# Loop 1 of a two-layer graph network: node sums over 32 nodes for each pair of tiles, in place of 128 nodes for each step of eight tiles

## The reference

```python
# layer 0, for each edge e from src to dst; w from a small MLP of the edge's length
w  = mlp(emb(edge_weight)).reshape(-1, 4, 32)
Y1 = sqrt(3) * edge_vec / |edge_vec|            # the edge's direction, 3 components
ss, vv = xs[src], xv[src]                       # 32 scalars, 32 vectors of 3
m0 = w[:, 0] * ss
m1 = w[:, 1][:, :, None] * ss[:, :, None] * Y1[:, None, :]
m2 = w[:, 2][:, :, None] * vv
m3 = w[:, 3] * einsum('emc,ec->em', vv, Y1) / sqrt(3)
msg_s = segment_sum(concat([m0, m3], 1), dst)   # sums over the edges of a node
msg_v = segment_sum(concat([m1, m2], 1), dst)
x = layernorm(x + concat([msg_s @ W_out0, msg_v . W_out1]) / 16)
```

## Time and profile before

| | |
|---|---|
| median of 3 runs | 2822.83 us (2813.37 to 2848.79) |
| profiled execution | 2817.75 us |
| its span, first to last instruction | 2815.9 us |
| mean granted clock of TensorE | 0.799 of full speed |
| TensorE matmul / weight load busy | 1998.1 / 1548.5 us |
| VectorE, ScalarE, GpSimd busy | 1563.1, 818.1, 1632.6 us |
| loop 1, by VectorE's first and last L805 | 70 to 1423 us |

### The profile page before, as it was taken

One profiled execution on the slowest core, in us unless ns is written; L12 is line 12 of the kernel. 1 busy time (PEld: TensorE's weight loads), 2 busy tenths in 40 slices (PEclk: granted clock), 3 DMA queues, 4 the chain that ended last, 5 costly groups with the idle time before them and its releaser, 6 DMA issues. The chain is left out here.

```text
span 2815.9 us, 38846 instructions
## 1 busy us (share of the span) xinstructions
PE 1998.1 (71%) x10027; PEld 1548.5 (55%) x10027; DVE 1563.1 (56%) x3820; ACT 818.1 (29%) x1930; POOL 1632.6 (58%) x1680
## 2 busy tenths in 40 slices
PE   6776878788888787888866556665566666566666
PEld 3554555555556465656545445555556555555555
DVE  6564455445445454556445436665566666566666
ACT  5111112112112112112124324343344434334443
POOL 6665654556656465566644555566556666665662
PEclk7787888888878888889877877777777777777878
DMA  8311222212222122222246543443343434333441
GB/s 265 92 44 37 60 56 63 60 54 63 59 59 65 50 60 56 67 60 71 69 119 166 135 120 89 93 94 92 86 97 94 95 91 95 92 88 93 95 97 46
DMA packets 221609, 238.19 MB, mean 85 GB/s; under 512 B 73212, under 2 KB 163240, under 8 KB 221131
## 3 DMA queue, kind: packets, MB, share of 16 engines
q0 software_dynamic: 53472, 110.50, 17.2%
q1 hardware_dynamic: 79835, 71.35, 8.3%
q10 hardware_dynamic: 88256, 55.83, 8.0%
HBM read 191.88 MB, written 45.62 MB: 84 GB/s over the span
## 5 line engine op out<-in xcount | busy, mean ns | idle before, releaser
L731 POOL DMA_INDIRECT gx<-node_d,idx x815 | 821.8, 1008 | 557.2 <-issue 245.5
L731 POOL DMA_INDIRECT gp<-p_tab_d,idx x831 | 787.8, 948 | 567.4 <-issue 281.8
L1096 PEld LDWEIGHTS ps_a<-hot,msg 128*128 128x128 f32 x3324 | 457.2, 214 | 205.7 <-issue 189.9
L1096 PE MATMUL ps_a<-hot,msg 128*128 128x128 f32 x3324 | 485.0, 302 | 52.2 <-issue 43.6
L2128 PE MATMUL ps_e<-win,hot_x 128*128 128x129 f32 x1664 | 319.8, 359 | 253.7 <-issue 163.3
L2128 PEld LDWEIGHTS ps_e<-win,hot_x 128*128 128x128 f32 x1664 | 289.1, 264 | 285.3 <-issue 199.5
L192 ACT ACTIVATE h<-ps_h,b 128x512 f32<-128x512 f32 x208 | 142.9, 687 | 750.1 <-remote 435.3
L2265 DVE TENSOR_TENSOR hot_x<-key_row,ps_s 128x1024 f32<-128x1024 bf16 x104 | 126.4, 1216 | 308.5 <-remote 263.1
L2217 PE MATMUL ps_g<-hot,hid 128*128 128x128 f32 x1664 | 239.5, 294 | 73.5 <-issue 71.5
L2013 ACT ACTIVATE hid<-hid,score 128x128 f32<-128x128 f32 x832 | 277.5, 393 | 10.1
L2217 PEld LDWEIGHTS ps_g<-hot,hid 128*128 128x128 f32 x1664 | 229.0, 209 | 90.0 <-issue 82.9
(11 more groups left out here) (303 smaller groups left out, 2425.4 us busy)
## 6 DMA issues: line engine op xcount, KB each, us to landing
win<-q_tab_d ACTq DMA_DIRECT2D x408, 64.5 KB
key_row<-key_row_d ACTq DMA_DIRECT2D x100, 256.0 KB
gp<-p_tab_d,idx POOLq DMA_INDIRECT x831
gx<-node_d,idx POOLq DMA_INDIRECT x815
p_tab_d<-acc SPq DMA_DIRECT2D x23, 516.0 KB
q_tab_d<-unit_area SPq DMA_DIRECT2D x36, 258.0 KB
q_tab_d<-acc SPq DMA_DIRECT2D x5, 774.0 KB, 4.1
emb<-emb_d SPq DMA_DIRECT2D x102, 32.0 KB
```

The costliest lines, as they stand in the source:

```text
L731: e.indirect_dma_start(out=buf[:, h, t, :], out_offset=None, in_=table, in_offset=bass.IndirectOffsetOnAxis(ap=idx[:, h, t:t + 1], axis=0) ...
L1096: last = e.matmul(ps_a[:, h, b, :], msgs[h].tile(t, b), hot[:, h, t, :], start=t == tiles.start, stop=t == tiles.stop - 1)
```

## The change

- The one-hot matrix of a tile is 32 wide (`WIN`) and not 128, and is made from `k["dloc"]`, which is relative to the start of the edge's pair.
- The matmuls of `sums` have 32 moving columns and not 128; the pair t // 2 has its own 32 columns of the half's 128 in the same bank, and each pair is a group of accumulation of its own.
- `add` loads four starts and adds four blocks of 2 x 32 columns to the accumulator, each waiting for the one before (`pair_own`), where it added one block of 2 x 128. The last step's two parts add two pairs each.
- `w["dloc"]`, its one subtraction in `prepare` and its count of edges outside go; layer 2's count, with the same blocks, is taken for both.

```diff
-        dloc=m.sb("dloc0", [P, LTILES]),
...
-                own.did(e.tensor_tensor(w["dloc"][:].rearrange(pairs, t=TPS), dstf[:].rearrange(pairs, t=TPS),
-                                        spread(of_step, 2, TPS), ALU.subtract))
...
-        hot = m.sb("hot0", [P, 2, TPS, P])
+        hot = m.sb("hot0", [P, 2, TPS, WIN])
...
                 def sums(h, b, tiles=slice(0, TPS)):
                     for t in range(tiles.start, tiles.stop):
-                        last = e.matmul(ps_a[:, h, b, :], msgs[h].tile(t, b), hot[:, h, t, :], start=t == tiles.start,
-                                        stop=t == tiles.stop - 1)
+                        last = e.matmul(ps_a[:, h, b, t // 2 * WIN:(t // 2 + 1) * WIN], msgs[h].tile(t, b), hot[:, h, t, :],
+                                        start=t % 2 == 0, stop=t % 2 == 1 or t == tiles.stop - 1)
...
                 def one_hot(j, h):
-                    e.tensor_tensor(hot[:, h], spread(ps_a[:, h, IOTA, :], 1, TPS),
-                                    spread(w["dloc"][:, bass.ds(j * TPS, TPS)], 2, P), ALU.is_equal)
-
-                def add(j, h, part=0):
-
-                    e.load([reg], k["start"][0:1, bass.ds(j * PPS, 1)])
-                    at = acc[:, :, bass.ds(e.snap(reg, min_val=0, max_val=N), P)]
+                    e.tensor_tensor(hot[:, h], spread(ps_a[:, h, IOTA, 0:WIN], 1, TPS),
+                                    spread(k["dloc"][:, bass.ds(j * TPS, TPS)], 2, WIN), ALU.is_equal)
+
+                def add(j, h, part=0, pairs=range(PPS)):
+
+                    starts = run_starts(e, k, j, regs)
                     e.wait_ge(sum_mm, j + (1 + part))
-                    e.wait_ge(acc_own, j + (2 + part))
-                    e.tensor_tensor(at, at, ps_a[:, h, 0:2, :], ALU.add).then_inc(acc_own, 1)
+                    for p in pairs:
+                        at = acc[:, :, bass.ds(starts[p], WIN)]
+                        if p == pairs.start:
+                            e.wait_ge(acc_own, j + (2 + part))
+                        else:
+                            e.wait_ge(pair_own, j * (PPS - 1) + (p - part))
+                        last = e.tensor_tensor(at, at, ps_a[:, h, 0:2, p * WIN:(p + 1) * WIN], ALU.add)
+                        last.then_inc(acc_own if p == pairs.stop - 1 else pair_own, 1)
...
-                in_block(own_w, w["dloc"], P)
                 messages(0, 3)
-                count(own_w, 0)
                 messages(1, 0)
-                in_block(own_w, k["dloc"], WIN)
+                in_block(own_w)
                 messages(1, 1)
-                count(own_w, 1)
+                count(own_w)
```

More of the change, by code:

```diff
@@ L608, in _ @@
                 pairs = "p (g t) -> p g t"
-                of_step = startf[:].rearrange("p (j q) -> p j q", q=PPS)[:, :, 0]
                 own.then(e.scalar_tensor_tensor(startf[:], past, float(BOUND), startf[:], ALU.min, ALU.max))
@@ L862, in edges0 @@
             m.sem(n) for n in ("used", "half_ok", "plain_ok", "ws_ok", "own0", "sum_mm", "acc_own"))
+        pair_own = m.sem("pair_own")
         later_ld, iota_ok, w_ok, w_own, sums_ok = (m.sem(n) for n in ("later_ld", "iota_ok", "w_ok", "w_own0",
@@ L1235, in _ @@
             def _(e):
-                reg = e.alloc_register("sum0_start")
+                regs = start_registers(e, "sum0")
                 def one_hot(j, h):
-                    e.tensor_tensor(hot[:, h], spread(ps_a[:, h, IOTA, :], 1, TPS),
-                                    spread(w["dloc"][:, bass.ds(j * TPS, TPS)], 2, P), ALU.is_equal)
-                def add(j, h, part=0):
-                    e.load([reg], k["start"][0:1, bass.ds(j * PPS, 1)])
-                    at = acc[:, :, bass.ds(e.snap(reg, min_val=0, max_val=N), P)]
-                    e.wait_ge(sum_mm, j + (1 + part))
-                    e.wait_ge(acc_own, j + (2 + part))
-                    e.tensor_tensor(at, at, ps_a[:, h, 0:2, :], ALU.add).then_inc(acc_own, 1)
+                    e.tensor_tensor(hot[:, h], spread(ps_a[:, h, IOTA, 0:WIN], 1, TPS),
+                                    spread(k["dloc"][:, bass.ds(j * TPS, TPS)], 2, WIN), ALU.is_equal)
+                def add(j, h, part=0, pairs=range(PPS)):
+                    starts = run_starts(e, k, j, regs)
+                    e.wait_ge(sum_mm, j + (1 + part))
+                    for p in pairs:
[6 more added lines that the diff above has]
+                        last.then_inc(acc_own if p == pairs.stop - 1 else pair_own, 1)
                 def residual(x1, out, x_in, x_value, done, tiles):
@@ L1284, in table_out, with in_block, count @@
                     e.tensor_tensor(v["p_buf"][:, t, 0:HW], bank[:, 0:HW], v["bias_r"], ALU.add).then_inc(p_even, 1)
[L1286 to L1291, removed]
+                def in_block(own_w):
+                    own_w.then(e.tensor_scalar(hit[:], k["dloc"][:], 0.0, None, ALU.is_ge))
+                    own_w.then(e.scalar_tensor_tensor(hit[:], k["dloc"][:], float(WIN), hit[:], ALU.is_lt, ALU.mult))
+                def count(own_w):
+                    own_w.then(e.tensor_reduce(n_hit[:, 0:1], hit[:, 0:TILES], AX.X, ALU.add))
+                    own_w.then(e.tensor_copy(n_hit[:, 1:2], n_hit[:, 0:1]))
                 def keys(own_w):
@@ L1440, in _ @@
                 residual(v["x1_e"][:, TWO, :], ps_a[:, 0, 0:END - 1, :], v["x_in_e"][:, TWO, :], (pad_st, 32), UNITS, TWO)
-                add(STEPS - 1, 1)
+                add(STEPS - 1, 1, 0, range(0, FIRST_PART // 2))
                 last_second(1)
@@ L1444, in _ @@
                 table_out(UNITS - 1, 1, unit_bank[2])
-                add(STEPS - 1, 1, 1)
+                add(STEPS - 1, 1, 1, range(FIRST_PART // 2, PPS))
                 residual(v["x1_e"][:, ONE, :], ps_a[:, 0, 0:1, :], v["x_in_e"][:, ONE, :], (pad_st, 32), UNITS + 1, ONE)
```

## The result

The changed kernel takes 2896.95 us, median of 4 runs (2888.59 to 2912.76), beside 2832.06 us for the kernel before on the same chip (4 runs, 2813.37 to 2848.79): a ratio of 1.0212, with a 95% interval of 1.0159 to 1.0265 (a ratio here is the one on record for the fast runs, which is not exactly the quotient of the two medians). That is 65 us slower, 46 us above the predicted 2851 and inside the range. The profiled execution took 2898.71 us, and its loop 1, from the first L801 to the last, 1423.4 us for 103 steps, 13.82 us each; before, with L805, it was 1352.2 us and 13.13 us. So loop 1 holds 71 us of the 81 us between the two profiled executions.

The account below looks back on a forecast made before the run. TensorE was taken to bound loop 1. A lower clock (+29 us) and one-time savings (-1) gave +28 us on the profiled 2817.75, that is 2846, and 2851 with the 5 us by which the median stands above; range 2755 to 2915.

Parts of the forecast that it names:

- the step on the clock: Loop 1's granted clock falls from 0.84 to about 0.76; forecast wrong if it stays 0.84 or falls to 0.70.
- The sums' pace is the loads': In loop 1's sums, weight loads stay near 0.11 us apart at 2.4 GHz, so fewer columns save next to nothing there.
- The rival in which the loads do not limit: Sums fall to a quarter, 4.56 to 1.14 us a step; GpSimd stops the gain at -275 us, 2548; chance 0.08.
- So loop 1 goes by TensorE.: TensorE bounds loop 1, with work for 10.73 us of a 13.04 us step at a mean clock of 0.84.
- it changes nothing: Late completions and instructions, not columns, pace loop 1's step: -5 to +10 us; chance 0.08.
- may come down from 0.21 to 0.167: Spacing in us of the sums' loads at 1.2 GHz; with the lower clock, the sums change by -0.18 us a step.
- the rival of 0.22: Loop 1's clock stays, as the gate may look at loads too: 2765 to 2782 us; chance 0.22.
- I take the columns as the likelier, 0.76.: Streaming columns set loop 1's clock, 0.84 to about 0.76; the rest of TensorE's step costs +0.65 us.
- the last matmuls: Last matmuls of the two halves of the sums end sooner with fewer columns: 0.08 us a step saved.
- I take 0.7: Share of TensorE's +0.39 us a step that reaches loop 1's step length: +29 us of +41.
- VectorE costs nothing: One-hot -0.79 us, four adds +0.7 us a step in loop 1, covered by TensorE's other work: 0.
- The slower rival: Thin half 1, `first` and half 0 bring loop 1's clock down to 0.70: 2910 to 2947 us; chance 0.15.

Follow-up runs that it names:

- load64: The changed kernel with 64 of the 128 stationary columns in each matmul of the sums, half of the output's features left out: 2822.1 us in one run.
- cols16_3: The changed kernel with 16 moving columns in the sums in place of 32, half of each pair's nodes left out: 2827.03 us in one run.
- before32: The kernel before with only its sums' matmuls cut to the first 32 one-hot columns, one-hot and add as before: 2334.91 us, ratio 1.0757.
- before_again: The kernel before, unchanged, run once more with a profile in the second comparison: 2805.18 us in one run.
- after_again: The changed kernel itself, measured again in the second comparison against the kernel before: 2841.72 us, ratio 1.015.
- cols96_3: The changed kernel with 96 moving columns in its sums, the 32 real ones and two repeats: 2820.99 us, ratio 1.0055 to the kernel before.
- half0wide_3: The changed kernel with 128 moving columns in half 0 of the sums and 32 in half 1: 2827.82 us, ratio 1.0064 to the kernel before.
- after_3: The changed kernel itself, measured once more in the third comparison against the kernel before: 2841.24 us, ratio 1.0129.
- one_add: The changed kernel with one add in place of four, the sums of three pairs of four left out: 2338.63 us, ratio 1.0768 to the kernel before.
- cols128: The changed kernel with 128 moving columns in its sums, the 32 real ones and three repeats: 2179.02 us, ratio 1.0039 to the kernel before.

## Why the prediction was right, and where it was not

The time lies in the range, but the step on the clock failed by the prediction's own sign: it called the forecast wrong if the clock of loop 1 "falls to 0.70", and 0.70 is what it fell to. The forecast was +28 us; the change cost 65 us where the result was measured, 38 and 40 us in the other two comparisons. That it came this near is in part luck: what the lower clock costs TensorE was put much too low, and what share of that reaches the step much too high.

**The sums' pace is the loads'.** Right. With 128, 96, 64, 32 and 16 moving columns the loads of a stream start 111 to 112 ns apart at 2.4 GHz, and with half the stationary columns 58. The rival in which the loads do not limit falls, by `load64` and `cols16_3`.

**"So loop 1 goes by TensorE."** The runs bear it out in full only for 32 columns with completions in time: `before32` has TensorE busy for 900.00 of 900 us and costs 7.6%. Where completions are late, as in the profile that was predicted from, it holds in part. In the eight traces of the second and third comparisons loop 1 took 1347 to 1387 us, while TensorE's work in the stretch went from 712 to 833 us. The rival "it changes nothing", which had the step paced by late completions, saw this, but is wrong on the time: the change costs 38 to 65 us in all three measurements.

**At 1.2 GHz the pace "may come down from 0.21 to 0.167".** Wrong: it stays 0.213. The two lone loads of L1109 were a poor guide, since a stream of 16 shows the pace and a pair shows one gap. The Trainium skill, "TensorE: Matmul & The Clock Gate", section "LDWEIGHTS (loading the stationary operand)", has a load cost its columns / 1.2 ns, 107 ns for 128 and 53 for 64; the runs agree at 2.4 GHz (111 and 58) and show twice as much at 1.2 GHz (213 and 107), so for these float32 loads the figure holds at the full clock only.

**The clock follows the columns that stream.** The direction was right, and the runs show it: 0.95, 0.87, 0.77 for 128, 64 and 32 columns on one chip, 0.84, 0.80, 0.71 for 128 (the kernel before), 96 and 32 on the others, with one and the same number of matmuls and loads a step; half as long a load leaves it at 0.69. So the clock does not stay, and the rival of 0.22 falls. It is not in proportion to the columns either: 16 give the same 0.71 as 32.

**"I take the columns as the likelier, 0.76."** This is the term that was mis-sized: it measured 0.70 to 0.71. Loop 2's row, at 62% busy, was no measure for loop 1, and the estimate spread the loss evenly over the step. It isn't even. With 900 / 13.13 = 68.5 and 900 / 13.82 = 65.1 steps in the stretch, TensorE's busy time a step goes from 740.09 / 68.5 = 10.80 to 815.56 / 65.1 = 12.52 us, +1.72 where the forecast had +0.39:

- the sums 314.5 / 68.5 = 4.59 to 307.3 / 65.1 = 4.72 us, +0.13 (forecast -0.18, and -0.08 for the last matmuls);
- `layer0_third` 169.2 / 68.5 = 2.47 to 233.9 / 65.1 = 3.59 us, +1.12. Spread evenly, 0.76 would have given 2.47 x 0.84 / 0.76 - 2.47 = +0.26;
- all else +0.47 (forecast +0.39, the +0.65 less these 0.26).

The mean clock of a stretch prices no single line: the sums, which bring the clock down, still start at full clock in 74% of cases, and `layer0_third` behind them pays.

**"I take 0.7" for what reaches the step.** Also off, the other way: the step grew by 0.69 of the 1.72 us, 0.40. Nor is 0.40 a constant: from `before_again` to `after_again`, reckoned alike, TensorE's step grows by 1.75 us (10.54 to 12.30) and the step by 0.23 (13.07 to 13.30), 0.13. Forecast +0.39 x 0.7, measured +1.72 x 0.40; the product is 0.27 against 0.69 us, times 103 = 28 and 71 us. What absorbs the rest goes with the lateness of completions, as the prediction suspected: it shrinks from 246 to 85 us in loop 1. Where TensorE has less work it is longer again: 262 us with 712 us of work in the stretch (`load64`), 245 with 750 (`cols96_3`), 166 with 780 (`half0wide_3`), 87 with 826 (`after_3`). The likely reading, not shown by itself, is that a longer TensorE ends at a time when the late signal would have come anyway. Where completions are in time nothing absorbs it: `before32` costs 164 us, 7.6%, against 38 to 65 us for the change itself in the three measurements with late ones (2841.72 - 2803.38, 2841.24 - 2801.22, 2896.95 - 2832.06). The changed kernel itself was not run on the chip of 2171 us; `before32` and `one_add` stand for it.

**VectorE costs nothing.** Right. The one-hot measures 418 ns (forecast 425), an add 222 (220), and four adds take 1.29 us from first to last in the timeline (forecast 1.1). `cols128` has them all and costs 8 us; `one_add` has a quarter of them and gains nothing over `before32`. In the trace after TensorE never waits for L817: it ends at 709.12 and half 1's first load stands at 715.68 in the timeline after, a cover of 6.6 us.

**The slower rival.** Its clock, 0.70, is the one measured, and its place too: the clock is won back in `layer0_third`, at that line's cost. Its picture of why, that half 1, `first` and half 0 count as one thin stretch in which any wait is enough, is not borne out as a whole: most falls come with no wait at all, and one wide half, which should have broken the stretch up, restored half of the clock (`half0wide_3`). Its time, 2910 to 2947, was too high because it too had 0.7 or all reach the step; the result lies between forecast and rival.

**Still open.** What makes the completions late, everywhere but on the chip of the first comparison, was not found. Nothing in the kernel was seen to set it. The same kernel before stands some 630 to 660 us apart on the two kinds of chip, far more than the change is worth, and no run shows how much of that is the late completions. How few columns a step keep the full clock was not narrowed down beyond the points above.

No version tried beats the kernel before: with 128 columns the changed code is 0.4% slower, and every narrower one is slower still. On the chip where completions are in time the step of `cols128`, 9.91 us, is close to what eight gathers take GpSimd:

```profile
L727 POOL DMA_INDIRECT gx<-node_d,idx x617 | 599.3, 971 | 188.1 <-issue 183.5 <-PE ps_h L196 3.7 <-DMA idx<-in_src 0.6
```

(599.3 + 183.5) / 617 = 1.27 us each, 10.1 us for eight, so nothing that TensorE saves there would show. VectorE's first product waits there for the gathered rows, and half 0 of the sums in turn for VectorE:

```profile
DVE vy L804 <- DMA gx<-node_d,idx: 228.6, 72, 5.7
...
PEld ps_a L1095 <- DVE msg L810: 85.3, 53, 3.5
```

With 128 columns on that chip loop 1 thus goes by the gathers, and with 32 by TensorE.

## What to carry to other kernels

Where each float32 matmul brings its own 128 x 128 weights, the load sets the pace, and cutting the moving columns below 128 saves no time. In this kernel it took away what kept TensorE at its full clock, and the bill came to the wide matmuls behind. So look at a line's own min/median/max before and after, not at the mean clock of the stretch. And ask how much of a longer engine its waits absorb: the edit cost 1.3 to 2.1% on chips with late completions, and its like, `before32` and `one_add`, 7.6 to 7.7% where they were in time.

## What the runs showed of the hardware

- The granted clock can fall while the profile, whose matmul ends are modelled, shows TensorE 100% busy, matmul behind matmul (703.40 to 713.60 us above; all 67 falls of `before32` from 300 to 1100 us).
- One kernel took 2171 us on one chip and 2801 to 2832 us elsewhere. In the traces taken elsewhere completions of TensorE reach VectorE late, in `before_again` with idleness of up to 18.8 us ahead of L805; in the four traces of variants on the fast chip they don't.
- Going from 32 to 16 moving columns changed neither the clock (0.71) nor the pace (0.111 and 0.21 us).
- Where completions were late, 120 us less work for TensorE in 900 shortened loop 1 by 10 us (`load64` against `after_again`).
- A float32 load of 64 stationary columns paces a stream at 58 ns (2.4 GHz) and 107 ns (1.2 GHz), one of 128 at 111 and 213 ns.
